# First batch's maxima split into two halves of eight heads, its second score pass started after the first half, GpSimd's bias sums moved behind its masks

## The chip, the cores and the metric

The kernel runs on one core of a Trainium2 chip. The metric is the device time of one execution in microseconds (us). The core's engines each run their own queue of instructions in order and wait for each other by semaphores: TensorE (PE in the rows; PEld is its loading of weights), VectorE (DVE), ScalarE (ACT), GpSimd (POOL) and SyncE (SP), which only starts DMAs. A trailing q (ACTq, SPq) marks the start of a DMA.

## The reference

The computation is one transformer layer on x of shape 8 x 256 x 256 (batch, token, feature), float32: cross attention to a context, then a layer of experts.

```python
scores = jnp.einsum('bihd,bjhd->bhij', qh, kh) * scale       # 16 heads of 16
keep = (j < i) | (i == 0) & (j == 0)
scores = jnp.where(keep, scores, jnp.float32(-jnp.inf))
probs = jax.nn.softmax(scores, axis=-1)
attn = jnp.einsum('bhij,bjhd->bihd', probs, vh).reshape(B, S, HID)
return attn @ W_o + b_o
...
x = x + _L0_xattn_ref(_layernorm(x), ctx, ctx, W_q, W_k, W_v, b_v, W_o, b_o)
x = x + _L0_ffn_ref(_layernorm(x), wg, w1, b1, w2, b2)       # top 2 of 8 experts, capacity 512
```

## The kernel before, in words

The attention part handles one batch per step, steps -2 to 8, as a software pipeline: in step s TensorE projects queries and keys of batch s+2, makes the maxima of batch s+1, and does the scores, exponentials and products with V of batch s. The order on every engine is written out by hand, in the `step` function of each engine's block and in the calls ahead of `steps(step)`; the first batch's maxima are in the calls ahead, its scores in step 0.

Queries and keys are cut into bf16 parts whose rows are stacked by DMAs into the buffers `Qs` and `Ks` (three of each; some share memory with expert weights, so the trace calls them `w_hi` and `w_lo`). A first score pass, `a_scores(s, pair)` (lines 1063 and 1066), puts twelve units of scores of batch s+1 into two banks in turn; units 0 to 5 are heads 0 to 7, units 6 to 11 heads 8 to 15. VectorE takes each unit's row maxima, negated (`maxima`, line 758); TensorE may score into a bank again when its maxima are taken.

`split_maxima` (lines 812, 814) then splits the 2 x 16 maxima per row into a bf16 part and the rest, TensorE turns them (`turn_maxima`, line 1161), ScalarE copies the result (`copy_maxima`, line 592) and starts a DMA (line 594) that puts them as two more rows into `Qs`. Since `Ks` holds ones in these rows, the second pass, `b_scores(s, g)` (lines 1079, 1082; four heads per group g), gives scores minus their maxima, which ScalarE's `exp` (line 525) turns into probabilities. GpSimd zeroes what the mask drops (`mask`, lines 395 to 397) and TensorE multiplies by V (`values`, lines 1098, 1099). The second pass uses banks 3 to 5; in the first batches bank 3 also takes the projected values of batch 0, which `add_value_bias(0)` moves into V with the bias added (line 775). Ahead of that it waits for V's ones, the extra column that yields the softmax's sum:

```python
dve.wait_ge(v_done, s + 2)
if first(s, 1):
    dve.wait_ge(ones_ready, s + 2)
```

`buffer_constants(q)` raises `ones_ready` on GpSimd (lines 315, 317). In GpSimd's queue, `buffer_constants(1)` follows `norm_powers(2)`, `fill_keys(2)` and `zero_queries(2)` (lines 320, 323: a memset of 128 x 2048 each); behind it come the context's split (line 404), the sums of x and the output's bias (`add_bias`, line 389) and the constants of the routing.

Of the kernel before, what the change touches and what calls it, by code (L numbers as in the profile page):

```python
# [6 lines left out]
P = 128  # L7
# [38 lines left out]
def attention(nc, sem, sb, persist, x, ctx_in, Wq, Wk, Wv, bv, Wo, bo, wg, w1, b1, w2, b2, xn_rows, out):  # L46
# [66 lines left out]
    nm_s = sb("nm_s", [P, 2, 2, HEADS], BF16)  # L113
    nmT = sb("nmT", [2 * HEADS, S], BF16)
    PT = [sb(f"PT{g}", [P, HPG * (S + P)], F32) for g in range(2)]
    OT = sb("OT", [P, GROUPS, S], F32)
# [42 lines left out]

    a_done, max_done, nm_ready, nmT_done, nmT_ready = (sem(n) for n in ("a_done", "max_done", "nm_ready", "nmT_done", "nmT_ready"))  # L160
    b_done, exp_done, mask_done, av_done, ot_ready = (sem(n) for n in ("b_done", "exp_done", "mask_done", "av_done", "ot_ready"))

# [73 lines left out]
    with block:  # L236
# [71 lines left out]
        def _(pool):  # L308
# [104 lines left out]
            def step(s):  # L413
                if s == 0:
                    add_bias(2)
                    mask(0, 0)
                    split_queries(0)
                    mask(0, 1)
                    split_keys(0)
                    mask(0, 2)  # L420
                    mask(0, 3)
                    norm_powers(3)
                    return
                if 0 < s < B - 2:
                    if s + 3 < B:
                        norm_powers(s + 3)
                    add_bias(s + 2)
                    split_context(s)
                    mask(s, 0)
                    mask(s, 1)  # L430
                    powers(s - 1, ln2_stats, mv2, ve2, rs2, ln2_pow)
                    split_keys(s)
                    mask(s, 2)
                    split_queries(s)
                    mask(s, 3)
                    return
# [38 lines left out]
            split_context(0)  # L475
            add_bias(0)
            add_bias(1)
            routing_constants()
            steps(step)
# [3 lines left out]
        def _(act):  # L483
# [104 lines left out]
            def copy_maxima(s):  # L588
                act.wait_ge(nmT_done, s + 2)
                if not first(s, 0):  # L590
                    act.wait_ge(max_stacked, 16 * (s + 1))
                act.activation(nmT[:, :], bank[1][0:2 * HEADS, 0:S], ACT.Copy).then_inc(nmT_ready, 1)
                wait_alone(act, started, nmT_ready, s + 2)
                act.dma_start(Qs[(s + 1) % BUFS][ROWS:ROWS + 2, :, :], nmT[:, :]).then_inc(max_stacked, 16)

            def step(s):
# [47 lines left out]
                else:  # L644
# [7 lines left out]
                    if proj_part(s) and s > 0:  # L652
                        round_x(s)
                    if s == 0:
                        round_queries(s)
                        exp(s, 0)
                        round_keys(s)
                        exp(s, 1)
                    elif score_part(s):
                        exp(s, 0)  # L660
                        exp(s, 1)
# [35 lines left out]
            round_queries(-1)  # L697
            round_context(0)
            norm_x(2)
            round_x(0)  # L700
            copy_maxima(-1)
            steps(step)

        @block.vector
        def _(dve):
# [46 lines left out]
            def unit_maxima(s, lo, hi):  # L752
                for u in range(lo, hi):
                    dve.wait_ge(a_done, UNITS * (s + 1) + u + 1)
                    if u == 0 and not first(s, 0):
                        dve.wait_ge(nm_ready, 2 * (s + 1))
# [46 lines left out]
            def logits(s):  # L803
                copy_logits(s)
                top_two(s - 1)

            def split_maxima(s):

                dve.wait_ge(max_done, UNITS * (s + 2))
                if not first(s, 0):  # L810
                    dve.wait_ge(nmT_done, s + 1)
                dve.tensor_copy(nm_s[:, :, 0, :], nm[:, :, :]).then_inc(nm_ready, 1)
                dve.wait_ge(nm_ready, 2 * (s + 1) + 1)
                dve.tensor_tensor(nm_s[:, :, 1, :], nm[:, :, :], nm_s[:, :, 0, :], ALU.subtract).then_inc(nm_ready, 1)
# [83 lines left out]
            def step(s):  # L898
# [71 lines left out]
                elif s == 0:  # L970
                    maxima(s, 0)
                    maxima(s, 1)
                    split_queries(s)
                    next_stats(s)
# [57 lines left out]
            next_stats(-1)  # L1032
            maxima(-1, 2)
            maxima(-1, 3)
            maxima(-1, 4)
            maxima(-1, 5)
            split_maxima(-1)
            add_value_bias(0)
            split_x(0)
# [5 lines left out]
        def _(pe):  # L1045
# [23 lines left out]
            def b_scores(s, g):  # L1069

                if g == 0:
                    pe.wait_ge(max_stacked, 16 * (s + 1))
                    if s == 0:
                        pe.wait_ge(v_ready, 2)
# [28 lines left out]
            def turn_values(s, t):  # L1103

                if t == 0:
                    pe.wait_ge(ot_ready, 2 * s)
                    if not (s > B - 1):
                        pe.wait_ge(nmT_ready, s + 1)
# [45 lines left out]
            def turn_maxima(s):  # L1154
                pe.wait_ge(nm_ready, 2 * (s + 2))
                if out_part(s):
# [3 lines left out]
                for t in range(2):  # L1160
                    last = pe.matmul(bank[1][0:2 * HEADS, t * P:(t + 1) * P], nm_s[:, t].rearrange("p a h -> p (a h)"), identb[:, :],
                                     start=True, stop=True)
                last.then_inc(nmT_done, 1)

            def project_turned(to, n, hi, lo, done):
# [21 lines left out]
            def queries(s):  # L1187
# [3 lines left out]
                elif out_part(s):  # L1191
                    pe.wait_ge(x2_ready, s)
                elif s == 0:
                    pe.wait_ge(nmT_ready, 1)
                project_turned(query_bank(s), 0, xT_hi, xT_lo, q_done)
# [72 lines left out]
            def step(s):  # L1268
                if s == B:
# [10 lines left out]
                    early_table(1, 1)  # L1280
                elif s == 0:
                    a_scores(s, 0)
                    queries(s)
                    b_scores(s, 0)
                    a_scores(s, 1)
                    keys(s)
                    b_scores(s, 1)
                    a_scores(s, 2)
                    values(s, 0)
                    a_scores(s, 3)  # L1290
                    b_scores(s, 2)
                    values(s, 1)
                    a_scores(s, 4)
                    b_scores(s, 3)
                    a_scores(s, 5)
                    values(s, 2)
                    turn_maxima(s)
# [131 lines left out]
            a_scores(-1, 2)  # L1429
            a_scores(-1, 3)  # L1430
            a_scores(-1, 4)
            turn_x(0)
            a_scores(-1, 5)
            turn_maxima(-1)
            steps(step)


# [478 lines left out]
```

## Time and profile before

| | us |
|---|---|
| median of 3 runs | 420.01 (419.99 to 422.09) |
| the profiled execution | 420.47 |
| its span, first to last instruction | 418.7 |
| TensorE busy | 365.2 (87%) |
| VectorE busy | 293.7 (70%) |
| ScalarE busy | 187.9 (45%) |
| GpSimd busy | 213.3 (51%) |

The attention stage takes the first half of the span, the experts the second. Shares of busy time are means over both. In the timelines below, a time in brackets at a row's end is how long the engine stood idle before it, with the instruction that ended the wait; a row without it followed at once, or nearly. The granted clock, PEclk, is 1.00 at the 2.4 GHz level and 0.50 at 1.2 GHz.

### The profile page before, as it was taken

Reading aid. Unit: us, or ns where it says so; the run is one execution under the profiler, and the core shown is the slowest. Engines: PE = TensorE matmul, PEld = TensorE weight load, DVE = VectorE, ACT = ScalarE, POOL = GpSimd, SP = SyncE. Lnnn points to the kernel's source line nnn. Section 1 sums busy time; section 2 is a strip of 40 time slices with the busy share of each in tenths; the row PEclk is TensorE's granted clock in tenths of the full one; section 3 lists DMA queues with packets and bytes.
Section 4 is the critical chain, followed back from the end, with each engine's and each line's share of the span. In section 5 each row is a group of like instructions: output and inputs, shape, how many; then the busy total and the mean of one; then the engine's idle time right before and its main releaser. Section 6 shows DMA issues by size and latency. Waiting matters only on the chain. (4 is left out here: it accounts for less than half of the span.)

```text
span 418.7 us, 8190 instructions
## 1 busy us (share of the span) xinstructions
PE 365.2 (87%) x3030; PEld 313.2 (75%) x3030; DVE 293.7 (70%) x627; ACT 187.9 (45%) x258; POOL 213.3 (51%) x305
## 2 busy tenths in 40 slices
PE   3777899999999999776418999999999999999991
PEld 3646597878787876545416899989899999989891
DVE  6586788887877777747733777776778777776840
ACT  4424556566665646751203436263625335263400
POOL 8679876767675635250446008163453717060632
PEclk9999999999999999995556999999999999999996
DMA  7774717162615172313218009173463809140323
GB/s 213 223 204 154 216 33 198 41 192 56 175 44 160 39 215 100 120 51 114 52 43 300 10 3 271 44 231 85 156 155 92 224 17 274 27 58 2 37 27 36
DMA packets 38315, 49.15 MB, mean 117 GB/s; under 512 B 7138, under 2 KB 34180, under 8 KB 37252
## 3 DMA queue, kind: packets, MB, share of 16 engines
q1 hardware_dynamic: 29636, 34.93, 28.0%
q0 software_dynamic: 6144, 8.33, 10.7%
q10 hardware_dynamic: 2496, 5.38, 4.0%
q8 instruction: 24, 0.39, 0.4%
q14 instruction: 15, 0.12, 0.1%
HBM read 27.60 MB, written 8.41 MB: 86 GB/s over the span
## 5 line engine op out<-in xcount | busy, mean ns | idle before, releaser
L1585 POOL DMA_INDIRECT out_dram<-Y,scatter_idx x32 | 51.3, 1603 | 105.8 <-DVE Y L1741 90.4
L1628 ACT ACTIVATE hr<-ps,b_sb 128x512 f32<-128x512 f32 x64 | 43.2, 686 | 98.9 <-PE ps L1785 65.1
L758 DVE TENSOR_REDUCE nm<-ps 128x2 f32<-128x512 f32 (+1 forms) x96 | 62.4, 682 | 15.3 <-PE ps L1066 14.7
L1795 PE MATMUL ps<-w_hi,h_hi 128*128 128x256 f32 x224 | 63.1, 282 | 0.0
L1795 PE MATMUL ps<-w_lo,h_hi 128*128 128x256 f32 x224 | 62.5, 279 | 0.0
L1795 PE MATMUL ps<-w_hi,h_lo 128*128 128x256 f32 x224 | 62.4, 279 | 0.0
L525 ACT ACTIVATE PT<-ps 128x1536 f32<-128x1536 f32 x32 | 46.4, 1451 | 26.7 <-PE ps L1082 26.2
L1716 DVE CAST h_hi<-hr 128x512 fp32r<-128x512 f32 x60 | 27.4, 456 | 38.9 <-ACT hr L1628 38.8
L1785 PE MATMUL ps<-XT_hi,w_hi 128*128 128x512 f32 x128 | 51.4, 402 | 1.5 <-DVE XT_lo L1699 1.5
L1785 PE MATMUL ps<-XT_hi,w_lo 128*128 128x512 f32 x128 | 51.2, 400 | 0.0
L1785 PE MATMUL ps<-XT_lo,w_hi 128*128 128x512 f32 x128 | 51.1, 399 | 0.0
L1795 PEld LDWEIGHTS ps<-w_hi,h_lo 128*128 128x128 f32 x224 | 42.1, 188 | 1.6
L1795 PEld LDWEIGHTS ps<-w_hi,h_hi 128*128 128x128 f32 x224 | 42.0, 188 | 1.5
L1718 DVE TENSOR_TENSOR h_lo<-hr,h_hi 128x512 fp32r<-128x512 f32 x60 | 41.7, 696 | 2.1
L1795 PEld LDWEIGHTS ps<-w_lo,h_hi 128*128 128x128 f32 x224 | 42.2, 188 | 0.0
L1572 POOL DMA_INDIRECT Xg<-xn_rows,gather_idx x32 | 32.4, 1014 | 12.4 <-issue 9.4
L1066 PE MATMUL ps<-mask,identb 128*128 128x256 bf16 (+1 forms) x96 | 29.7, 309 | 0.0
L1785 PEld LDWEIGHTS ps<-XT_hi,w_hi 128*128 128x128 f32 x128 | 24.5, 192 | 5.8 <-issue 1.9
L1785 PEld LDWEIGHTS ps<-XT_lo,w_hi 128*128 128x128 f32 x128 | 24.5, 192 | 5.8
L1785 PEld LDWEIGHTS ps<-XT_hi,w_lo 128*128 128x128 f32 x128 | 24.6, 192 | 3.8
L395 POOL TENSOR_SCALAR_AFFINE_SELECT PT<-PT 128x4 f32<-128x4 f32 x32 | 6.5, 204 | 33.3 <-ACT PT L525 33.2
L1098 PE MATMUL ps<-PT,V 128*32 128x256 f32 x256 | 21.5, 398 | 0.8 <-POOL PT L397 0.7
(234 smaller groups left out, 886.3 us busy)
## 6 DMA issues: line engine op xcount, KB each, us to landing
raw<-in_L_ffn_w_dram SPq DMA_DIRECT2D x12, 1024.0 KB, 8.1
raw<-in_L_ffn_w_dram ACTq DMA_DIRECT2D x4, 1024.0 KB, 5.3
c_sb<-in_ctx_dram SPq DMA_DIRECT2D x8, 256.0 KB, 3.2
xn_rows<-x2n SPq DMA_DIRECT2D x8, 256.0 KB, 3.2
out_dram<-x_all SPq DMA_DIRECT2D x8, 256.0 KB, 2.9
x_all<-in_x_dram SPq DMA_DIRECT2D x1, 1280.0 KB, 6.6
w_lo<-k_h SPq DMA_DIRECT2D x9, 128.0 KB, 2.5
w_hi<-q_h SPq DMA_DIRECT2D x9, 128.0 KB, 2.5
```

Source lines behind the costliest of these rows:

```text
L395: pool.affine_select(p0[:, :, 0:1], p0[:, :, 0:1], [[0, HPG], [0, 1]], ALU.is_ge, 0.0, base=0, channel_multiplier=-1)
L525: act.activation(PT[g % 2][:, :], prob_score, ACT.Exp, scale=float(HD) ** -0.5).then_inc(exp_done, 1)
L758: dve.tensor_reduce(nm[:, tile, h:h + count], max_bank[u % 2].rearrange("p (h j) -> p h j", h=count), AX_X, ALU.max, negate=True).then_inc ...
L1066: pe.matmul(diag, identb[:, :], mask1[:, :, :] if tile else mask0[:, :, :], start=False, stop=True, skip_group_check=True).then_inc(a_done, 1)
L1098: pe.matmul(out, V[s % 2][:, 0, h, :], PT[g % 2][:, hh * S:(hh + 1) * S], start=True, stop=False)
L1572: pool.indirect_dma_start(Xg[q][:, j, :], None, xn_rows[:, :], bass.IndirectOffsetOnAxis(ap=gather_idx[:, ST * e + j:ST * e + j + 1], axis ...
L1585: pool.indirect_dma_start(out_rows[:, :], bass.IndirectOffsetOnAxis(ap=scatter_idx[:, ST * e + j:ST * e + j + 1], axis=0), Y[q][:, j, :], ...
L1628: act.activation(hr[c % 2][:, :], h_bank[c % 4], ACT.Relu, bias=b1_sb[q][:, c:c + 1]).then_inc(hr_ready, 1)
L1716: dve.tensor_copy(h_hi_of(e, c), hr[c % 2][:, :]).then_inc(hh_ready, 1)
L1718: dve.tensor_tensor(h_lo_of(e, c), hr[c % 2][:, :], h_hi_of(e, c).bitcast(F32), ALU.subtract).then_inc(hl_ready, 1)
L1785: last = pe.matmul(h_bank[c % 4], w[q][:, k, c, :], a[q][:, k, :], start=(n == 1), stop=(n == 6))
L1795: last = pe.matmul(y_bank[j // 2][:, (j % 2) * D:(j % 2 + 1) * D], a[c % 4][:, j * P:(j + 1) * P], w[q][:, c, :], start=(c == 0 and n == 0 ...
```

## The change

The first batch's maxima are split, turned and stacked in two halves. `split_half(0)` follows the sixth maximum and `split_half(1)` the twelfth; `turn_half` and `copy_half` do for eight heads what `turn_maxima` and `copy_maxima` do for sixteen, each with buffers and semaphores of its own. The second score pass of groups 0 and 1 waits for the first half's DMA, that of groups 2 and 3 for the second's. `add_value_bias(0)` is moved ahead of the second half's maxima, since `b_scores(0, 0)`, which writes over its bank, now comes earlier. The order of step 0 is written anew on TensorE, VectorE, ScalarE and GpSimd. GpSimd's `add_bias` of batches 0, 1 and 2 and its routing constants come later. In the other batches only the counts of the semaphores are one lower.

```diff
@@ pool.step @@
                 if s == 0:
-                    add_bias(2)
                     mask(0, 0)
+                    add_bias(0)
                     split_queries(0)
                     mask(0, 1)
                     split_keys(0)
                     mask(0, 2)
                     mask(0, 3)
                     norm_powers(3)
+                    add_bias(1)
+                    add_bias(2)
                     return
+                if s == B - 2:
+                    routing_constants()
@@ pool, ahead of the steps @@
             buffer_constants(1)
             split_context(0)
-            add_bias(0)
-            add_bias(1)
-            routing_constants()
             steps(step)
@@ act @@
+            def copy_half(n):
+                act.wait_ge(half_nmT_done, n + 1)
+                act.activation(nmT_half[n][:, :], bank[1][0:HEADS, n * S:(n + 1) * S], ACT.Copy).then_inc(half_nmT_ready, 1)
+                act.wait_ge(half_nmT_ready, n + 1)
+                act.dma_start(Qs[0][ROWS:ROWS + 2, n * HEADS // 2:(n + 1) * HEADS // 2, :], nmT_half[n][:, :]).then_inc(half_stacked[n], 16)
...
                     if s == 0:
+                        exp(s, 0)
+                        copy_half(1)
                         round_queries(s)
-                        exp(s, 0)
+                        exp(s, 1)
                         round_keys(s)
-                        exp(s, 1)
...
             round_context(0)
+            copy_half(0)
             norm_x(2)
             round_x(0)
-            copy_maxima(-1)
             steps(step)
@@ dve @@
+            def split_half(n):
+                heads = slice(n * HEADS // 2, (n + 1) * HEADS // 2)
+                dve.wait_ge(max_done, (n + 1) * UNITS // 2)
+                dve.tensor_copy(nm_half[:, n, :, 0, :], nm[:, :, heads]).then_inc(half_nm_ready, 1)
+                dve.wait_ge(half_nm_ready, 2 * n + 1)
+                dve.tensor_tensor(nm_half[:, n, :, 1, :], nm[:, :, heads], nm_half[:, n, :, 0, :], ALU.subtract).then_inc(half_nm_ready, 1)
...
                     maxima(s, 0)
+                    split_queries(s)
                     maxima(s, 1)
-                    split_queries(s)
...
             maxima(-1, 2)
+            split_half(0)
+            add_value_bias(0)
             maxima(-1, 3)
             maxima(-1, 4)
             maxima(-1, 5)
-            split_maxima(-1)
-            add_value_bias(0)
+            split_half(1)
             split_x(0)
             steps(step)
@@ pe @@
             def b_scores(s, g):
 
+                if s == 0 and g % 2 == 0:
+                    pe.wait_ge(half_stacked[g // 2], 16)
...
+            def turn_half(n):
+                pe.wait_ge(half_nm_ready, 2 * n + 2)
+                pe.wait_ge(k_rest_ready, 2)
+                if n == 1:
+                    pe.wait_ge(half_nmT_ready, 1)
+                for t in range(2):
+                    last = pe.matmul(bank[1][0:HEADS, n * S + t * P:n * S + (t + 1) * P], nm_half[:, n, t].rearrange("p a h -> p (a h)"), identb[:, :],
+                                     start=True, stop=True)
+                last.then_inc(half_nmT_done, 1)
...
             def queries(s):
                 elif s == 0:
-                    pe.wait_ge(nmT_ready, 1)
+                    pe.wait_ge(half_nmT_ready, 2)
...
                 elif s == 0:
+                    b_scores(s, 0)
+                    turn_half(1)
                     a_scores(s, 0)
                     queries(s)
-                    b_scores(s, 0)
+                    b_scores(s, 1)
                     a_scores(s, 1)
+                    values(s, 0)
                     keys(s)
-                    b_scores(s, 1)
                     a_scores(s, 2)
-                    values(s, 0)
+                    b_scores(s, 2)
                     a_scores(s, 3)
-                    b_scores(s, 2)
                     values(s, 1)
+                    b_scores(s, 3)
                     a_scores(s, 4)
-                    b_scores(s, 3)
+                    values(s, 2)
                     a_scores(s, 5)
-                    values(s, 2)
                     turn_maxima(s)
                     values(s, 3)
...
             a_scores(-1, 3)
+            turn_half(0)
             a_scores(-1, 4)
             turn_x(0)
             a_scores(-1, 5)
-            turn_maxima(-1)
             steps(step)
```

On VectorE the order around the first batch's maxima was this (the reduces write `nm`; the cast and the subtraction that follow make `nm_s`; the V row is the value bias, the last row the split of x):

```order
L758 TENSOR_REDUCE nm<-ps 128x2
L758 TENSOR_REDUCE nm<-ps 128x4
L758 TENSOR_REDUCE nm<-ps 128x2 x2
L758 TENSOR_REDUCE nm<-ps 128x4
L758 TENSOR_REDUCE nm<-ps 128x2 x2
L758 TENSOR_REDUCE nm<-ps 128x4
L812 CAST nm_s<-nm 128x2x16
L814 TENSOR_TENSOR nm_s<-nm,nm_s 128x2x16
L775 TENSOR_TENSOR V<-ps,bv_bc 128x32x16
L725 TENSOR_TENSOR xT_lo<-ps,xT_hi 128x512
```

The same place on VectorE is now, with line numbers of the changed kernel (its V row is again the value bias):

```order
L772 TENSOR_REDUCE nm<-ps 128x2
L772 TENSOR_REDUCE nm<-ps 128x4
L824 CAST nm_half<-nm 128x2x8
L826 TENSOR_TENSOR nm_half<-nm,nm_half 128x2x8
L789 TENSOR_TENSOR V<-ps,bv_bc 128x32x16
L772 TENSOR_REDUCE nm<-ps 128x2 x2
L772 TENSOR_REDUCE nm<-ps 128x4
L772 TENSOR_REDUCE nm<-ps 128x2 x2
L772 TENSOR_REDUCE nm<-ps 128x4
L824 CAST nm_half<-nm 128x2x8
L826 TENSOR_TENSOR nm_half<-nm,nm_half 128x2x8
L737 TENSOR_TENSOR xT_lo<-ps,xT_hi 128x512
```

The value bias has moved from behind the twelve maxima to behind the sixth, ahead of six reduces.

On TensorE, from the last scores of the first batch to the queries of step 0, the order was this (the row with `nm_s` turns the maxima, the rows with `Ks,Qs` and `mask` are the next batch's scores):

```order
L1063 MATMUL ps<-w_lo,w_hi 128x128 x4
L1066 MATMUL ps<-mask,identb 128x512
L1161 MATMUL ps<-identb,nm_s 32x128 x2
L1063 MATMUL ps<-Ks,Qs 128x256 x2
L1066 MATMUL ps<-mask,identb 128x2x128
L1063 MATMUL ps<-Ks,Qs 128x256 x2
L1066 MATMUL ps<-mask,identb 128x2x128
L1172 MATMUL ps<-xT_hi,w_hi 128x256
```

It is now this, where lines 1106 and 1109 are the second score pass of group 0 and line 1198 turns the second half:

```order
L1087 MATMUL ps<-w_lo,w_hi 128x128 x4
L1090 MATMUL ps<-mask,identb 128x512
L1106 MATMUL ps<-w_hi,w_lo 128x256 x4
L1109 MATMUL ps<-w_hi,w_lo 128x128 x4
L1198 MATMUL ps<-identb,nm_half 16x128 x2
L1087 MATMUL ps<-Ks,Qs 128x256 x2
L1090 MATMUL ps<-mask,identb 128x2x128
L1087 MATMUL ps<-Ks,Qs 128x256 x2
L1090 MATMUL ps<-mask,identb 128x2x128
L1209 MATMUL ps<-xT_hi,w_hi 128x256
```

The second pass of group 0 has moved ahead of the turning, of a pair of score units and of the queries' twelve matmuls.

## Rows read from the trace of the kernel before

**Rows 1.** Waits of TensorE, 49.8 to 150 us: total, times, longest.

```profile
PE ps L1079 <- DMA w_lo<-nmT: 0.9, 1, 0.9
```

**Rows 2.** Timeline of VectorE, 25 to 49 us: start, duration, instruction, [idle before].

```profile
25.80 3.94 DVE L758 TENSOR_REDUCE nm<-ps 128x2 f32<-128x512 f32 x6
...
30.04 1.29 DVE L758 TENSOR_REDUCE nm<-ps 128x2 f32<-128x512 f32 x2 [0.29 <-PE ps L1066]
...
32.02 0.69 DVE L775 TENSOR_TENSOR V<-ps,bv_bc 128x512 f32<-128x512 f32 x1
...
37.66 1.29 DVE L758 TENSOR_REDUCE nm<-ps 128x4 f32<-128x512 f32 x2 [3.15 <-PE ps L1066]
...
38.87 0.68 DVE L733 TENSOR_TENSOR q_rest<-ps,q_h 128x512 f32<-128x512 f32 x1
...
47.87 0.53 DVE L814 TENSOR_TENSOR nm_s<-nm,nm_s 128x32 bf16<-128x32 f32 x1
```

**Rows 3.** Timeline of GpSimd, 27 to 32 us, same columns.

```profile
27.72 1.80 POOL L320 MEMSET w_hi<- 128x2048 f32 x1
...
31.78 0.15 POOL L317 MEMSET V<- 128x32 f32 x1
```

**Rows 4.** Timeline of TensorE, 32 to 50 us, same columns.

```profile
32.04 0.28 PE L1161 MATMUL ps<-identb,nm_s 128*32 128x128 bf16 x2 [1.60 <-DVE nm_s L814]
...
33.37 0.38 PE L1172 MATMUL ps<-xT_hi,w_hi 128*128 128x256 f32 x1 [0.28 <-DVE xT_lo L725]
...
36.35 0.61 PE L1079 MATMUL ps<-w_hi,w_lo 128*128 128x256 bf16 x4 [1.30 <-DMA w_hi<-nmT]
...
37.71 0.36 PE L1172 MATMUL ps<-cT_hi,w_hi 128*128 128x256 f32 x1
...
39.21 0.61 PE L1079 MATMUL ps<-w_hi,w_lo 128*128 128x256 bf16 x4
...
41.56 0.39 PE L1063 MATMUL ps<-Ks,Qs 126*128 126x256 bf16 x2
...
46.96 0.66 PE L1098 MATMUL ps<-PT,V 128*32 128x256 f32 x8
...
48.45 0.29 PE L1161 MATMUL ps<-identb,nm_s 128*32 128x128 bf16 x2 [0.61 <-DVE nm_s L814]
...
49.01 0.66 PE L1098 MATMUL ps<-PT,V 128*32 128x256 f32 x8 [0.27 <-POOL PT L397]
...
49.82 0.39 PE L1183 MATMUL ps<-w_hi,cT_hi 128*128 128x256 f32 x1
```

**Rows 5.** Timeline of ScalarE, 32 to 38 us, same columns.

```profile
32.36 0.37 ACT L592 ACTIVATE nmT<-ps 32x256 bf16<-32x256 f32 x1 [2.06 <-PE ps L1161]
...
35.08 0.60 ACT L503 ACTIVATE q_h<-ps 128x512 bf16<-128x512 f32 x1 [2.35 <-PE ps L1172]
...
37.22 1.45 ACT L525 ACTIVATE PT<-ps 128x1536 f32<-128x1536 f32 x1 [1.54 <-PE ps L1082]
```

**Rows 6.** Timeline of GpSimd, 33 to 56 us, same columns.

```profile
33.10 2.51 POOL L389 TENSOR_TENSOR x_all<-x_all,bo_bc 128x512 f32<-128x512 f32 x2
...
43.36 0.61 POOL L330 CAST k_m<-k_rest 128x512 bf16<-128x512 f32 x1
...
45.49 0.20 POOL L395 TENSOR_SCALAR_AFFINE_SELECT PT<-PT 128x4 f32<-128x4 f32 x1
...
55.40 0.21 POOL L395 TENSOR_SCALAR_AFFINE_SELECT PT<-PT 128x4 f32<-128x4 f32 x1 [0.36 <-ACT PT L525]
```

**Rows 7.** Busy time by stretch: PE, PEld, DVE, ACT, POOL; PEclk, DMA share, GB/s.

```profile
17.90:20.90 3.00, 0.30 (x4) 0.10 (x3) 1.82 (x3) 0.00 (x0) 1.04 (x2) 1.00 0.77 196
...
184.00:186.00 2.00, 1.16 (x20) 0.69 (x18) 0.94 (x1) 1.73 (x2) 0.62 (x2) 1.00 0.76 262
...
186.00:188.00 2.00, 2.00 (x23) 1.53 (x23) 0.79 (x8) 0.00 (x0) 0.80 (x2) 0.64 0.00 0
```

**Rows 8.** Busy time by stretch, the experts' first matmuls, columns as before.

```profile
223.00:227.00 4.00, 4.00 (x10) 3.13 (x11) 0.97 (x4) 0.69 (x1) 2.82 (x4) 0.50 0.92 369
```

More of the change, by code:

```diff
@@ L114, in attention @@
     nmT = sb("nmT", [2 * HEADS, S], BF16)
+    nmT_half = [sb(f"nmT_half{n}", [HEADS, S], BF16) for n in range(2)]
+    nm_half = sb("nm_half", [P, 2, 2, 2, HEADS // 2], BF16)
     PT = [sb(f"PT{g}", [P, HPG * (S + P)], F32) for g in range(2)]
@@ L160, in attention @@
     a_done, max_done, nm_ready, nmT_done, nmT_ready = (sem(n) for n in ("a_done", "max_done", "nm_ready", "nmT_done", "nmT_ready"))
+    half_nm_ready, half_nmT_done, half_nmT_ready = sem("half_nm_ready"), sem("half_nmT_done"), sem("half_nmT_ready")
+    half_stacked = [sem(f"half_stacked{n}") for n in range(2)]
     b_done, exp_done, mask_done, av_done, ot_ready = (sem(n) for n in ("b_done", "exp_done", "mask_done", "av_done", "ot_ready"))
@@ L588, in copy_maxima @@
             def copy_maxima(s):
-                act.wait_ge(nmT_done, s + 2)
-                if not first(s, 0):
-                    act.wait_ge(max_stacked, 16 * (s + 1))
+                act.wait_ge(nmT_done, s + 1)
+                if s > 0:
+                    act.wait_ge(max_stacked, 16 * s)
                 act.activation(nmT[:, :], bank[1][0:2 * HEADS, 0:S], ACT.Copy).then_inc(nmT_ready, 1)
-                wait_alone(act, started, nmT_ready, s + 2)
+                wait_alone(act, started, nmT_ready, s + 1)
                 act.dma_start(Qs[(s + 1) % BUFS][ROWS:ROWS + 2, :, :], nmT[:, :]).then_inc(max_stacked, 16)
+            def copy_half(n):
[3 more added lines that the diff above has]
+                act.dma_start(Qs[0][ROWS:ROWS + 2, n * HEADS // 2:(n + 1) * HEADS // 2, :], nmT_half[n][:, :]).then_inc(half_stacked[n], 16)
             def step(s):
@@ L754, in unit_maxima @@
                     dve.wait_ge(a_done, UNITS * (s + 1) + u + 1)
-                    if u == 0 and not first(s, 0):
-                        dve.wait_ge(nm_ready, 2 * (s + 1))
+                    if u == 0 and s == 0:
+                        dve.wait_ge(half_nm_ready, 4)
+                    if u == 0 and s > 0:
+                        dve.wait_ge(nm_ready, 2 * s)
                     tile, h, count = max_unit(u)
@@ L805, in logits @@
                 top_two(s - 1)
+            def split_half(n):
[4 more added lines that the diff above has]
+                dve.tensor_tensor(nm_half[:, n, :, 1, :], nm[:, :, heads], nm_half[:, n, :, 0, :], ALU.subtract).then_inc(half_nm_ready, 1)
             def split_maxima(s):
                 dve.wait_ge(max_done, UNITS * (s + 2))
-                if not first(s, 0):
-                    dve.wait_ge(nmT_done, s + 1)
+                if s == 0:
+                    dve.wait_ge(half_nmT_done, 2)
+                else:
+                    dve.wait_ge(nmT_done, s)
                 dve.tensor_copy(nm_s[:, :, 0, :], nm[:, :, :]).then_inc(nm_ready, 1)
-                dve.wait_ge(nm_ready, 2 * (s + 1) + 1)
+                dve.wait_ge(nm_ready, 2 * s + 1)
                 dve.tensor_tensor(nm_s[:, :, 1, :], nm[:, :, :], nm_s[:, :, 0, :], ALU.subtract).then_inc(nm_ready, 1)
@@ L1069, in b_scores @@
             def b_scores(s, g):
+                if s == 0 and g % 2 == 0:
+                    pe.wait_ge(half_stacked[g // 2], 16)
                 if g == 0:
-                    pe.wait_ge(max_stacked, 16 * (s + 1))
+                    if s > 0:
+                        pe.wait_ge(max_stacked, 16 * s)
                     if s == 0:
@@ L1107, in turn_values @@
                     if not (s > B - 1):
-                        pe.wait_ge(nmT_ready, s + 1)
+                        pe.wait_ge(nmT_ready, s)
                 elif max_part(s):
@@ L1154, in turn_maxima @@
             def turn_maxima(s):
-                pe.wait_ge(nm_ready, 2 * (s + 2))
+                pe.wait_ge(nm_ready, 2 * (s + 1))
                 if out_part(s):
```

## The prediction, on record before the changed kernel ran

> **What bounds the kernel now.** I read the table of stages first, then the waits of TensorE, then the timelines of the engines around the change. From the second batch on TensorE hardly waits: between 49.8 and 150 us its longest wait is 0.9 us [rows 1]. So the attention stage from 50 us on runs at TensorE's pace, and whatever the first batch's step ends earlier or later by reaches the end of the span nearly whole. The change lies before that, between 27 and 50 us, where TensorE does wait: 1.60 us for the split maxima, then 1.30 us for the DMA that stacks them [rows 4]. VectorE waits there once, 3.15 us, and from 37.66 on its queue runs without a gap until 47.87 + 0.53 = 48.40 [rows 2]: 10.74 us of work.
>
> I call the units of the first batch's maxima u6 to u11 in its second half, b(0,g) the second score pass of group g in step 0, and "end of step 0" the first values projection of step 1, at 49.82 [rows 4].
>
> **The change part by part.**
>
> *Splitting by halves, and the V bias.* On VectorE the first half's split stands behind the sixth maximum, and right behind it now stands the addition of the value bias into V, ahead of u6. This addition waits for `ones_ready`, which GpSimd raises with its second filling of V's ones. The filling isn't moved: it starts at 31.78 and takes 0.15, so it is done at 31.93; ahead of it GpSimd runs two large memsets, of 1.80 us each, the first from 27.72 [rows 3]. Those start when the norm's powers are done, which hang on statistics whose place on VectorE is the same. In the kernel before, the addition started at 32.02, and the wait was met by then [rows 2].
>
> Now VectorE is there at about 27.8 (the six maxima from 25.80 take 3.94, so the second of them ends at 27.11; the split pair behind it is my estimate of 0.7). It stands until 31.95, over 4 us, and behind it in its queue are u6 to u11, for which TensorE waits: each of its score units but the next two needs a bank that a maximum frees. With the addition's 0.69, u6 starts at 32.65 instead of 27.11: **5.5 us later**. Everything up to the second half's turning moves with it: u11 ends at 31.33 + 5.5 = 36.85, the second turning is at 32.04 + 5.5 = 37.55. TensorE is done with the last scores at 32.04 - 1.60 + 5.5 = 35.95 and starts b(0,0) there, 0.4 before the 36.35 of before. The first half's rows are long in place: from turning to b(0,0) it was 36.35 - 32.04 = 4.31 [rows 4], so from 27.9 they land at 32.2. This is all that the early half gains.
>
> *The second half's copy.* It stands behind exp(0,0) on ScalarE, and queries(0) wait for it. Exp started 37.22 - 36.35 = 0.87 behind b(0,0) and takes 1.45; the copy took 0.37 [rows 5]. So: 35.95 + 0.87 + 1.45 + 0.37 = 38.65, queries at 38.7 instead of 33.37. A projection of this size takes 39.21 - 37.71 = 1.5 [rows 4], so b(0,1) starts at 40.2 (before 39.21), and the rounded queries come 35.08 - 33.37 = 1.71 later and take 0.60: at 41.0. VectorE's split of the queries starts at 41.05; before, 38.87 [rows 2].
>
> *What follows in step 0.* Two bounds. From below: with no further wait, the 10.74 us of VectorE run from 41.05 to 51.8 (the two maxima that stood ahead of the queries' split are behind it now, so all of it counts), and the turning that was at 48.45 is at 51.85. Before, the last products waited 0.27 for their mask behind that turning [rows 4]; that wait goes, so step 0 ends 3.4 - 0.27 = 3.1 later. From above, the chain through the keys: they now stand behind b(0,1), a pair of score units and a group of products, a set that took 41.56 - 39.21 = 2.35 [rows 4]. So keys at 42.55, the next pair of scores at 44.05, its first unit 0.4 later (half of a third of 2.35, an estimate) at 44.45; VectorE would have been there before, so it waits. Two maxima (1.31) and the keys' split (0.68, as the queries') end at 46.45; GpSimd's mask of the third group starts 45.49 - 43.36 = 2.13 behind its first piece of the keys [rows 6], at 48.6, and the products 46.96 - 45.49 = 1.47 behind that, at 50.1 instead of 46.96. The last pair of scores is now behind these products: 0.8 + 0.4 (thirds of 2.35 again), then the last two maxima, which in the first batch started 2.00 before their turning (30.04 to 32.04): 51.3 + 2.0 = 53.3, against 48.45, or 4.85 - 0.27 = 4.6 at the end of step 0. Consecutive instructions overlap by about 0.1, which this addition counts in several places, so I take **4.4**, near the upper end.
>
> *The clock.* During VectorE's stop TensorE has nothing but the small turning of the first half from about 27.6 to 33.3. A stretch of 3.00 us with 0.30 busy left the granted clock at 1.00 (the 2.4 GHz level); later 1.16 busy of 2.00 us was followed by a fall to 0.50 (1.2 GHz), the mean of the next 2 us being 0.64 [rows 7]. This stop would be nearly twice the first of these stretches and emptier than the second, so I expect the fall. Once down, TensorE was busy for 4.00 us of 4.00 and still at 0.50 [rows 8]. Half rate over such a stretch loses at most 2.0; at least 0, if the clock holds. Part of it lies under VectorE's maxima, but b(0,0) and the turning of x don't, so I take **1.5**, towards the upper end. The Trainium skill, page "TensorE: Matmul & The Clock Gate", section "HAM oscillation — how this bites in real kernels", says that a matmul burst after a long wait begins throttled, every time; by it the fall is sure and the sum is the one above, and the first of rows 7 speaks neither for nor against it, being shorter.
>
> *Edits that I cost at nothing.* GpSimd's bias sums for batches 1 and 2, 2.51 us for two [rows 6], go behind the norm's powers at the end of step 0. GpSimd leaves its masks some 2.5 later than before (its third is 3.1 late, and the fourth had had to wait a little), plus 2.51, so it comes to the first mask of step 1 about 5.0 later; that mask had 0.36 of wait for exp, and exp itself comes 4.4 later, so 0.2 is left, ahead of products that stand behind a projection; without this cover it would be those 2.51. The first bias sum, half of 2.51, stands behind the first mask, where GpSimd waits for the queries' remainder anyway. The routing constants go to the last step but one, into GpSimd's wait for that step's first exp. One DMA issue and a copy more on ScalarE lie in its waits before the norm and before the rounded queries. The first half's two VectorE instructions lie inside the stop.
>
> **Sum.** 4.4 + 1.5 = 5.9. The profiled execution took 420.47; with it 426.4. It lies 0.46 above the median of 420.01, so the forecast is **425.9**.
>
> **The rivals.**
>
> *The clock holds.* For it: 0.30 busy in 3.00 us did nothing [rows 7]. Against: the length of this stop. Time: 420.0 + 4.4 = 424.4.
>
> *The clock falls again at the end of step 0.* There TensorE waits for the third mask and for the last maxima, and a thin stretch preceded the fall at 186 [rows 7]. Step 1, which TensorE bounds, would then begin at half rate: 2.0 more [rows 8], 427.9. Against: in the same place before, it held with somewhat fewer waits.
>
> *VectorE is never behind.* The chain through the keys finds slack that I don't see, and only VectorE's 10.74 us count: 3.1 and no clock, 423.1.
>
> *The other side: V's ones are there in time.* If GpSimd's two memsets were much shorter with VectorE standing still, VectorE would pass the addition at 27.8, u6 would start at 28.5, 1.4 late; b(0,0) would wait for its rows until 32.2, the queries come at 34.95, their split on VectorE at 37.3, and 10.74 later, 48.05, the turning: 0.4 earlier, and 0.27: 419.3. Each us of stop costs one us, so it is later than before from 0.7 us of stop on. For it: nothing but that the early half is there to be used. Against: the memset took 1.80 [rows 3], and both would have to vanish.
>
> **How the numbers follow.** Forecast 0.42, clock holds 0.27, clock falls twice 0.16, VectorE's floor 0.08, ones in time 0.05, 0.02 for anything else. Half a per cent, 2.1 us, is about what a measurement here can tell from no change. All cases but the fifth lie over 422.1: slower 0.93. The fifth gives 419.3 at its best, which is inside: same 0.05, faster 0.02. The range from 422.8 to 428.4 holds the floor, the forecast and the second fall with half a us to spare on either side.
>
> **What would show it.** In the profile after: an idle time of about 4 us on VectorE before the line that adds the value bias, at 32 us, put down to GpSimd's memset of V; TensorE without scores from 28 to 33 us; b(0,0) at about 36, queries near 38.7 (later, if the clock fell: then PEclk is 0.50 from some 32 us to 38); the end of step 0 at 54 to 56 instead of 49.82; from there every stage shifted alike. The prediction is wrong if VectorE does not stop there, if step 1 starts before 52, or if a later stage gives time back.

## The result, and the profile after

The changed kernel took 425.68 us (median of 6 runs, 423.36 to 429.64); the kernel before, run beside it, 422.05 (419.99 to 424.29). The ratio is 1.0103, 95% interval [1.0068, 1.0139]: on 420.01 us, 4.3 us slower (2.9 to 5.8). The forecast was 425.9, which is 5.9 slower. The profiled execution took 423.36, span 421.6.

Times ahead of the change differ between executions (the third pair of the first batch's maxima starts at 25.40 here, at 25.80 in before [rows 2]). So I count from the start of that pair, called **u4**; each such time is from one profiled execution. The end of step 0 (the first values projection of step 1) lies 24.02 behind u4 in before, 29.27 in after: **5.25 us later**.

VectorE after, timeline from 25 us on (start, duration, instruction, idle before and its releaser):

```profile
25.40 1.25 DVE L772 TENSOR_REDUCE nm<-ps 128x2 f32<-128x512 f32 x2
...
26.89 0.17 DVE L826 TENSOR_TENSOR nm_half<-nm,nm_half 128x16 bf16<-128x16 f32 x1
31.62 0.69 DVE L789 TENSOR_TENSOR V<-ps,bv_bc 128x512 f32<-128x512 f32 x1 [4.56 <-POOL V L321]
32.23 1.28 DVE L772 TENSOR_REDUCE nm<-ps 128x2 f32<-128x512 f32 x2
...
```

The stop is there: VectorE stands 4.56 us ahead of the value bias, and the seventh maximum, u6, starts at 32.23, 6.83 behind u4. In before it came 1.31 behind [rows 2]. What it waits for stands in GpSimd's timeline of after:

```profile
27.31 1.80 POOL L324 MEMSET w_hi<- 128x2048 f32 x1
29.06 1.81 POOL L327 MEMSET w_lo<- 128x2048 f32 x1
30.80 0.53 POOL L319 MEMSET V<- 128x512 f32 x1
31.38 0.15 POOL L321 MEMSET V<- 128x32 f32 x1
...
42.09 0.61 POOL L334 CAST q_m<-q_rest 128x512 bf16<-128x512 f32 x1 [0.62 <-DVE q_rest L745]
...
46.87 0.61 POOL L334 CAST k_m<-k_rest 128x512 bf16<-128x512 f32 x1 [1.54 <-DVE k_rest L745]
...
60.45 0.21 POOL L399 TENSOR_SCALAR_AFFINE_SELECT PT<-PT 128x4 f32<-128x4 f32 x1
```

The two large memsets still stand ahead of V's ones, as in before [rows 3]. The last row is step 1's first mask: no wait is listed, and GpSimd comes to it late, but no wait of TensorE for it follows (below). TensorE after, timeline 27 to 55 us:

```profile
27.14 0.28 PE L1198 MATMUL ps<-identb,nm_half 128*16 128x128 bf16 x2
32.97 0.61 PE L1087 MATMUL ps<-w_lo,w_hi 126*128 126x128 bf16 x4 [5.55 <-DVE nm L772]
...
36.35 0.60 PE L1106 MATMUL ps<-w_hi,w_lo 128*128 128x256 bf16 x4
...
37.87 0.28 PE L1198 MATMUL ps<-identb,nm_half 128*16 128x128 bf16 x2 [0.70 <-DVE nm_half L826]
...
39.06 0.36 PE L1209 MATMUL ps<-xT_hi,w_hi 128*128 128x256 f32 x1
...
40.51 0.61 PE L1106 MATMUL ps<-w_hi,w_lo 128*128 128x256 bf16 x4
...
50.60 0.66 PE L1125 MATMUL ps<-PT,V 128*32 128x256 f32 x8 [1.47 <-POOL PT L401]
...
53.74 0.28 PE L1188 MATMUL ps<-identb,nm_s 128*32 128x128 bf16 x2 [1.38 <-DVE nm_s L837]
...
54.67 0.39 PE L1220 MATMUL ps<-w_hi,cT_hi 128*128 128x256 f32 x1
```

Of the waits of before that the halves were to shorten [rows 4], the 1.30 for the stacking DMA is gone, and of the 1.60 for the split 0.70 is left. In their place stands one of 5.55, and in step 0 one of 1.47 for the third mask (none before) and one of 1.38 for the last maxima (0.61 before). The clock, by stretches of after (TensorE, weight load, VectorE, ScalarE, GpSimd busy; granted clock; DMA share, GB/s):

```profile
28.00:32.00 4.00, 0.00 (x0) 0.00 (x0) 0.38 (x1) 1.09 (x2) 3.94 (x5) 0.63 0.89 265
32.00:36.00 4.00, 3.03 (x17) 2.41 (x18) 2.84 (x5) 0.46 (x1) 0.74 (x1) 0.52 0.57 187
36.00:40.00 4.00, 3.16 (x30) 2.40 (x29) 3.53 (x7) 1.84 (x3) 1.20 (x3) 1.00 0.01 2
40.00:55.00 15.00, 12.15 (x148) 8.88 (x148) 11.34 (x24) 6.52 (x7) 12.22 (x21) 1.00 0.66 177
```

It fell during the stop to the lower level (1.2 GHz), held there through three of the four score units that were left, and was back at 36. It did not fall again before 55. From step 1 on (53 to 153 us) TensorE waits as little as before [rows 1]. Apart from the wait at 53.74, the longest is:

```profile
PE ps L1106 <- DMA w_lo<-nmT: 0.4, 1, 0.4
```

### The profile page after: what moved, and what is told of

The parts are those of the page before. It is cut to its first block and busy times, and to the rows that moved or that the text cites. A ratio compares the mean times of both kernels' runs of the same rounds, so it can differ in the third digit from the quotient of the medians.

```text
span 421.6 us, 8198 instructions
## 1 busy us (share of the span) xinstructions
PE 364.1 (86%) x3032; PEld 312.6 (74%) x3032; DVE 293.6 (70%) x629; ACT 188.3 (45%) x259; POOL 213.6 (51%) x305
## 5 line engine op out<-in xcount | busy, mean ns | idle before, releaser
L772 DVE TENSOR_REDUCE nm<-ps 128x2 f32<-128x512 f32 (+1 forms) x96 | 62.3, 681 | 14.4 <-PE ps L1090 14.0
L1087 PE MATMUL ps<-w_lo,w_hi 126*128 126x256 bf16 (+1 forms) x96 | 14.3, 256 | 10.1 <-DVE nm L772 7.0
```

The costliest lines, as they stand in the source:

```text
L1087: pe.matmul(max_bank[u % 2][:, h * width:(h + 1) * width], Q[0:ROWS, h0 + h, tile * P:(tile + 1) * P], K[0:ROWS, h0 + h, 0:width], start=( ...
```

## The experiments

A time "behind u4" can be compared between kernels; a ratio is against the kernel before, run beside it on the same chip.

**1. V's ones early.** GpSimd fills them ahead of the norm's powers and of the two large memsets; the rest is as after.

```diff
             split_queries(-1)
+            buffer_constants(1)
             norm_powers(2)
...
             zero_queries(2)
-            buffer_constants(1)
             split_context(0)
```

> The changed kernel with one call moved: GpSimd fills V's ones for batch 1 before the third norm's powers instead of behind its two large memsets. If VectorE's stop at the value bias is what costs, the stop is gone, the sixth maximum is followed by the second half within 1.5 us, the clock stays at 1.00, and step 1 begins at 49.1 to 50.6 us of the span (54.67 in the changed kernel, 49.82 before); the time is within 0.3% of the kernel before. If it is the new order of step 0 that costs, step 1 still begins at 52 us or later.

Measured: 423.94 us, ratio 1.0011 [0.9975, 1.0047]. VectorE has no stop any more (its timeline):

```profile
28.44 0.17 DVE L826 TENSOR_TENSOR nm_half<-nm,nm_half 128x16 bf16<-128x16 f32 x1
28.55 0.69 DVE L789 TENSOR_TENSOR V<-ps,bv_bc 128x512 f32<-128x512 f32 x1
```

But the end of step 0 is 27.02 behind u4: 2.25 less than in after, and still 3.00 later than before. It lies at 53.97 of the span, past the 52 that was the sign for the new order. TensorE's timeline shows two reasons:

```profile
28.69 0.28 PE L1198 MATMUL ps<-identb,nm_half 128*16 128x128 bf16 x2
...
34.98 1.03 PE L1106 MATMUL ps<-w_hi,w_lo 128*128 128x256 bf16 x4 [1.58 <-DMA w_hi<-nmT_half]
...
49.91 0.66 PE L1125 MATMUL ps<-PT,V 128*32 128x256 f32 x8 [1.47 <-POOL PT L401]
...
53.05 0.28 PE L1188 MATMUL ps<-identb,nm_s 128*32 128x128 bf16 x2 [1.38 <-DVE nm_s L837]
```

The half's rows need 34.98 - 28.69 = 6.29 from turning to use, where before needed 4.31 [rows 4], and the clock falls about the end of that wait:

```profile
31.00:34.00 3.00, 1.43 (x12) 1.04 (x12) 1.84 (x4) 1.52 (x3) 2.63 (x2) 1.00 0.99 339
34.00:38.00 4.00, 3.02 (x16) 1.78 (x16) 1.69 (x5) 1.52 (x2) 0.00 (x0) 0.58 0.28 72
```

(Stretches of the same execution; the DMA engines are 0.99 busy in the first. That this delays the rows fits, but was not tried by itself; in experiment 8 the rows were in use 4.56 after the turning.) And the new order's waits of 1.47 and 1.38 are the same as in after. The stop was the largest single cause that was taken out, not the only one. (The ratio's interval ends at 2.0 us, under the 3.00 of this one execution; how often the clock falls there is not known.)

**2. The stop with TensorE kept busy.** After, with 23 matmuls into an unused bank while VectorE stands.

```diff
             turn_half(0)
+            for _ in range(23):
+                pe.matmul(ps[:, 4, :], identb[:, :], mask0[:, :, :].rearrange("p h j -> p (h j)"), start=True, stop=True)
             a_scores(-1, 4)
```

> The changed kernel with 23 unused matmuls of 128x512 on TensorE during VectorE's stop, into a bank that is free then. If the fall of the clock costs what was predicted, the granted clock stays at 1.00 from 27 to 37 us and step 1 begins 1.0 to 1.8 us earlier than 54.67. If the fall lies wholly under VectorE's maxima, step 1 begins within 0.3 us of 54.67.

Measured: 428.23 us, ratio 1.0072 [1.0027, 1.0118]. Its clock around the stop, columns as above:

```profile
29.00:37.00 8.00, 6.71 (x36) 2.96 (x36) 3.38 (x9) 1.46 (x3) 6.67 (x9) 1.00 0.60 181
```

VectorE's stop is as long, and behind it the six maxima run without a gap (its timeline):

```profile
35.23 0.69 DVE L789 TENSOR_TENSOR V<-ps,bv_bc 128x512 f32<-128x512 f32 x1 [4.55 <-POOL V L321]
35.84 4.08 DVE L772 TENSOR_REDUCE nm<-ps 128x2 f32<-128x512 f32 x6
```

The clock holds at 2.4 GHz, and the end of step 0 is 28.33 behind u4: 4.31 later than before. So of after's 5.25 the clock made 29.27 - 28.33 = **0.94**, a little under the 1.0 to 1.8 expected, and the stop and the order 4.31. (The profiled execution was the longest of this kernel's, 431.04 us, but from 26 us to the end of step 0 its granted clock is 1.00 throughout. The totals alone, 1.0072 and 1.0103, are too close to tell the two kernels apart.)

**3. The bias early, alone.** Before, with only the value bias moved ahead of the seventh maximum: no halves, no new order.

```diff
             maxima(-1, 2)
+            add_value_bias(0)
             maxima(-1, 3)
...
             split_maxima(-1)
-            add_value_bias(0)
             split_x(0)
```

> The kernel before, whole maxima and old order, with only the value bias moved ahead of the second half's maxima on VectorE. If the stop costs by itself, VectorE waits over 4 us for V's ones and step 1 begins at 53.5 to 56 us instead of 49.82. If the 3.15 us that VectorE waits later in the kernel before can take the stop up, step 1 begins before 51.5 us.

Measured: 426.7 us, ratio 1.0101 [1.0061, 1.0141], the same loss as the whole change. VectorE's stop, and then TensorE's timeline:

```profile
32.69 0.69 DVE L775 TENSOR_TENSOR V<-ps,bv_bc 128x512 f32<-128x512 f32 x1 [4.97 <-issue]
```

```profile
34.04 0.61 PE L1063 MATMUL ps<-w_lo,w_hi 126*128 126x128 bf16 x4 [5.75 <-DVE nm L758]
...
56.02 0.38 PE L1183 MATMUL ps<-w_hi,cT_hi 128*128 128x256 f32 x1
```

"issue" names no releaser; GpSimd's memset of V's ones runs from 32.45 to 32.60, so it is the same wait. The clock falls here too (0.50 from 34 to 38 us). With u4 at 26.47, step 0 ends 5.53 later. One moved line is enough to make the loss.

**4. GpSimd's moves, alone.** Before, with `add_bias(0)` between the first mask and the queries' split, `add_bias(1)` and `(2)` behind `norm_powers(3)`, and the routing constants in the last step but one:

```diff
                 if s == 0:
-                    add_bias(2)
                     mask(0, 0)
+                    add_bias(0)
                     split_queries(0)
...
                     norm_powers(3)
+                    add_bias(1)
+                    add_bias(2)
                     return
...
```

> The kernel before with only GpSimd's bias sums and routing constants moved as in the change. If they are hidden, as predicted, step 1 begins at 49.6 to 50.1 us and its first products are not late. If the sums delay the masks or the next context's split, TensorE waits for GpSimd in step 0 or 1, by 0.8 to 2.5 us in all.

Measured: 424.62 us, ratio 1.003 [0.9991, 1.0068]; the end of step 0 is 1.84 later (25.86 behind u4). Where it shows on TensorE:

```profile
45.30 0.66 PE L1099 MATMUL ps<-PT,V 128*32 128x256 f32 x8 [2.09 <-POOL PT L397]
```

In before it was this:

```profile
43.47 0.66 PE L1098 MATMUL ps<-PT,V 128*32 128x256 f32 x8 [0.41 <-POOL PT L397]
```

In the old order GpSimd has no slack ahead of the queries' split, so `add_bias(0)` pushes its masks. In after it waits 0.62 and 1.54 at the two splits, and the same edit costs nothing there.

**5. The old waits filled, without halves.** Before, with the keys, and VectorE's statistics and splits, put into the wait for the DMA; GpSimd's splits ahead of its masks. TensorE's part:

```diff
                     queries(s)
+                    keys(s)
                     b_scores(s, 0)
                     a_scores(s, 1)
-                    keys(s)
                     b_scores(s, 1)
...
```

> The kernel before without any halves; only the order of step 0 is new: TensorE does the keys ahead of the second score pass, in the 1.30 us that it waits for the stacked maxima; VectorE does statistics and both splits in its 3.15 us of wait; GpSimd splits the queries ahead of the first mask; the bias sum of batch 2 and the routing constants come later. If step 0 is bound by waits that an order can fill, step 1 begins at 48.0 to 49.0 us (49.82 before) and the time falls by 0.2 to 0.4%. If only an earlier second pass can help, as the change has it, step 1 begins at 49.6 or later.

Measured: 422.5 us, ratio 1.0023 [0.9994, 1.0052]; 1.26 later at the end of step 0. The expectation missed: the wait for the DMA went, and these took its place (waits of TensorE, 34 to 53 us):

```profile
PE ps L1099 <- POOL PT L397: 2.0, 3, 0.9
PE ps L1080 <- ACT PT L526: 0.8, 1, 0.8
PE ps L1162 <- DVE nm_s L815: 0.8, 1, 0.8
```

Step 0 is paced by VectorE and GpSimd as well as by that wait; work put into it comes out behind it.

**6. After, once more**, with no edit.

> The changed kernel once more, beside the others on one chip. The first 6 runs gave a ratio of 1.0103, and its profile gave 2 us back between 186 and 204 us, where the clock fell later than in the profile before. If that gift belongs to the execution and not to the kernel, the mean ratio is near 1.012 (5.3 us at the end of step 0); if a later stage takes the delay up for good, it is at most 1.007.

Measured: 426.73 us, ratio 1.0109 [1.0069, 1.015]. This is nearer to the first expectation (1.012) than to the second (at most 1.007). The end of step 0 is again 29.27 behind u4, to the hundredth. What differs is the stretch from the last but one turning of x2 to the experts' first matmul, in which the attention ends and the routing is done. The first row is of after, the second of this execution, the third of before:

```profile
187.79:225.83 38.04, 16.79 (x158) 12.13 (x159) 22.06 (x72) 8.16 (x15) 14.07 (x19) 0.66 0.30 82
```

```profile
189.24:229.57 40.33, 20.17 (x158) 14.55 (x159) 22.17 (x72) 8.15 (x15) 14.04 (x19) 0.55 0.27 77
```

```profile
183.48:222.97 39.49, 18.82 (x158) 13.64 (x159) 22.18 (x72) 8.16 (x15) 14.06 (x20) 0.54 0.29 80
```

One program took 38.04 and 40.33 for the same 158 matmuls, at mean clocks of 0.66 and 0.55. So the 1.45 us that after's profile gives back there against before (39.49 - 38.04) can't be put down to the change. In this execution nothing is given back: its span is 425.4, 6.7 over the 418.7 of before.

**7 and 8. Halves with another step 0.** Both build on experiment 1, with `add_bias(0)` ahead of the first mask. In 7 the keys go ahead of the queries on every engine, the weights' split behind the maxima; in 8 step 0 has before's order from the queries on. TensorE's part of 7:

```diff
                     a_scores(s, 0)
-                    queries(s)
+                    keys(s)
                     b_scores(s, 1)
                     a_scores(s, 1)
+                    queries(s)
                     values(s, 0)
-                    keys(s)
                     a_scores(s, 2)
...
```

And of 8:

```diff
                     queries(s)
-                    b_scores(s, 1)
                     a_scores(s, 1)
-                    values(s, 0)
                     keys(s)
+                    b_scores(s, 1)
                     a_scores(s, 2)
-                    b_scores(s, 2)
+                    values(s, 0)
...
```

> The changed kernel with V's ones filled early (as in the first experiment) and step 0 ordered anew: keys ahead of the queries on all engines, so that TensorE has work while the second half's copy waits behind the first exp; the weights' split and a memset behind the maxima. If the halves are worth something once nothing waits for V's ones and the copy is covered, step 1 begins 22 to 23.5 us after the maxima of the third pair begin (24.02 before, 29.27 in the changed kernel). If the halves' DMA or VectorE's queue bounds it, 24 us or more.

> The changed kernel with V's ones filled early and, from the queries on, the order of step 0 of the kernel before on TensorE, ScalarE, VectorE and GpSimd. Between the end of the first group's scores, the first pair and the queries on TensorE and the start of step 1 lay 12.80 us before and 14.16 in the changed kernel. If the new order costs the 1.4 us between them, 12.6 to 13.1 here; if they come from the lateness of what stands ahead, 14 or more again.

Measured: 7 took 421.45 us, ratio 1.0007 [0.9979, 1.0035], end of step 0 23.81 behind u4 (0.21 earlier than before, between its two expectations); 8 took 423.99, ratio 1.0045 [1.0025, 1.0065], though its step 0 ends 23.02 behind u4, a whole 1.00 earlier. Once the queries, the second pass of group 0 and the first pair of score units are issued, the same work is left up to step 1 in all three orders: it took 54.67 - 40.51 = 14.16 in after, 49.82 - 37.02 = 12.80 in before and 49.03 - 36.53 = 12.50 in 8 (TensorE's timelines; one row of before, two of 8):

```profile
37.02 0.39 PE L1063 MATMUL ps<-Ks,Qs 126*128 126x128 bf16 x4
```

```profile
36.53 0.84 PE L1087 MATMUL ps<-Ks,Qs 126*128 126x128 bf16 x6
...
49.03 0.39 PE L1220 MATMUL ps<-w_hi,cT_hi 128*128 128x256 f32 x1
```

In experiments 1 and 2, which have after's order and other times ahead of it, the same work took 53.97 - 39.82 = 14.15 and 57.34 - 43.18 = 14.16. So the new order costs 1.4, and it is the order, not the halves nor the lateness of what stands ahead. But 8 pays in step 1 (its TensorE timeline):

```profile
53.67 0.38 PE L1087 MATMUL ps<-w_hi,w_lo 126*128 126x256 bf16 x2 [2.55 <-issue]
```

"issue" names no releaser. The last key transfer was started at 47.43, and the list of DMA issues, 30 to 60 us (KB each, median us to landing), puts its landing at 47.43 + 6.2 = 53.63, where TensorE starts:

```profile
raw<-in_L_ffn_w_dram ACTq DMA_DIRECT2D x1, 1024.0 KB, 9.3
...
w_hi<-k_l SPq DMA_DIRECT2D x1, 128.0 KB, 6.2
```

The first row is 1 MB of expert weights, started at 42.63, so it lands at 51.93, while that transfer is under way. The clock falls right behind TensorE's wait:

```profile
49.00:53.60 4.60, 2.12 (x20) 1.85 (x16) 1.28 (x3) 2.27 (x4) 4.14 (x7) 1.00 0.22 52
53.60:57.00 3.40, 3.33 (x21) 2.85 (x22) 1.44 (x4) 0.71 (x1) 2.95 (x4) 0.57 0.00 0
```

**9 to 11. That load later.** The 1 MB goes to the end of step 0 in 8 (run 9), in 7 (run 10) and in before (run 11, the control).

```diff
-                    if s in (0, B - 3):
-                        prefetch(s != 0)
+                    if s == B - 3:
+                        prefetch(1)
...
                     if max_part(s) and s > 0:
                         copy_maxima(s)
+                    if s == 0:
+                        prefetch(0)
```

> The halves with GpSimd's ones early and step 0 in its old order (the run before this one in its line), and now the 1 MB load of the experts' weights that ScalarE issues at 42.6, in the middle of step 0, comes after the last instruction of step 0 on ScalarE (about 48 to 49). Theory: step 1's first score pass waited 2.55 us at 53.67 for the second part of the stacked keys, whose last transfer took 6.2 us from issue to landing beside that load. Without it the transfers take 3 us or so, the wait is under 0.6, and the lead of 1.0 us at the end of step 0 is kept: the turning of x2 at 120.8 to 121.8 after the third pair's maxima (before 122.25, without the move 124.89), total 419.5 to 421.5 where before gives 422. Rival: the wait is the late split of the keys and not the load: it stays over 2 us, and the total is as without the move, 423.5 to 424.5.

> The halves with GpSimd's ones early and the keys ahead of the queries throughout, and the same load moved to the end of step 0. There the wait for the stacked queries at 53.16 was only 0.79. Theory: that wait goes and nothing else, so 0.5 to 1 us below the kernel without the move, total 420.5 to 421.5. Rival: no change within what a measurement tells (421.5 +- 1).

> The kernel before with the same load alone moved to the end of step 0: the control for the two others. Its step 1 waits only 0.2 us for stacked parts, so no change is expected: ratio 0.998 to 1.002. Rival: the load later gets in the way of step 1's own stacking, and the ratio is above 1.002.

Measured: 9 took 424.42 us, ratio 1.0048 [1.0008, 1.0087]; 10 took 423.57, 1.003 [0.9996, 1.0064]; 11 took 422.41, 0.9998 [0.996, 1.0035]. The mechanism is right: in 9 the key transfer lands in 2.4, and TensorE's wait of 2.55 in step 1 is gone:

```profile
raw<-in_L_ffn_w_dram ACTq DMA_DIRECT2D x1, 1024.0 KB, 4.8
...
w_hi<-k_l SPq DMA_DIRECT2D x1, 128.0 KB, 2.4
```

From step 1 to the first turning of x2 it takes 152.34 - 53.16 = 99.18, against 101.87 in 8 and 98.23 in before. The 0.95 over before is a new wait, for step 1's first mask (TensorE's timeline):

```profile
62.31 0.66 PE L1127 MATMUL ps<-PT,V 128*32 128x256 f32 x8 [0.95 <-POOL PT L401]
```

GpSimd works without a pause up to that mask, and in its queue stand the two bias sums, 2.52 us, that the change moved to the end of step 0. So where TensorE isn't late by something else, that edit shows (read from the rows; it was not tried by itself). In 10 this wait is 0.52.

The total I expected of 9, 419.5 to 421.5, is not there: it is the rival's (423.5 to 424.5), but not for the rival's reason. 10 lies over both ranges that were given for it, and 11 came as expected. The end of step 0 is 24.78 behind u4 in 9, 24.42 in 10 and 24.24 in 11. That of 9 is 1.76 later than in 8, with the same order ahead of it. The same stretch in 9 and (second row) in 8:

```profile
32.00:39.00 7.00, 6.24 (x31) 3.80 (x31) 4.30 (x8) 3.35 (x5) 4.37 (x5) 0.51 0.36 116
```

```profile
32.00:39.00 7.00, 5.86 (x56) 5.16 (x55) 5.72 (x11) 2.72 (x5) 3.34 (x5) 1.00 0.50 162
```

All of the 1.76 is there by the queries (9.03 behind u4 in 8, 39.18 - 28.38 = 10.80 in 9), before the moved load starts (53.33). Of the five profiled executions with V's ones early the clock fell about there in four (0.58 from 34 to 38 us in experiment 1 and from 31 to 35 in 7, 0.51 in 9, 0.50 from 32 to 37 in 10) and held only in 8. So the lead of 1.00 in 8 is that of the one execution in which it held. How often it falls is not known from one profile each, so why 9 and 10 gain nothing in the median stays open. No run beat the kernel before.

## Why the prediction was right

The mechanism held, and so did its chain, step by step. Times behind u4: as predicted without the clock term (the prediction's times less 25.80; for step 1 with the 4.4 that it took), as measured with the clock held (experiment 2), and in after:

| start of | predicted | clock held | after |
|---|---|---|---|
| value bias on VectorE | 6.15 | 6.22 | 6.22 |
| second pass of group 0 | 10.15 | 10.02 | 10.95 |
| queries | 12.9 | 12.72 | 13.66 |
| second pass of group 1 | 14.4 | 14.17 | 15.11 |
| third group's products | 24.3 | 24.26 | 25.20 |
| last turning | 27.5 | 27.40 | 28.34 |
| step 1 | 28.4 | 28.33 | 29.27 |

That the total came out at 425.68 against 425.9 is in part luck: the kernel before took 422.05 beside it, not the 420.01 that the forecast starts from, so the medians are 3.63 apart and not 5.9.

- *The stop*: over 4 us and u6 5.5 later were forecast; 4.56 and 6.83 - 1.31 = 5.52 measured. Experiment 1 removes the cause and the stop goes; experiment 3 makes it alone.
- *Step 0's order*: of the bounds 3.1 and 4.6 I took 4.4; with the clock held it was 4.31. The chain through the keys was the right one: the two waits that it gives, for the third mask and for the last maxima, are rows of after.
- *The clock*: the fall came, at the place named; its size failed. I took 1.5 of at most 2.0; it cost **0.94**. The low stretch in which TensorE had work ran only from 32.97 to about 36, not 4 us, and part of it lay under VectorE's maxima, which at full clock (experiment 2) set the pace there. What the Trainium skill says (page "TensorE: Matmul & The Clock Gate", section "HAM oscillation — how this bites in real kernels"), that a burst after a long wait begins throttled, fits after and experiments 3 and 6: behind waits of 5.55, 5.75 and 5.54 the clock was 0.52, 0.50 and 0.50.
- *Edits at nothing*: true where they stand. GpSimd came to step 1's first mask 5.45 later behind u4 than before (5.0 forecast), and no wait of TensorE followed. But the cover was the change's own lateness: by experiment 4 `add_bias(0)` costs 1.84 without the wait for the queries' remainder, and in 9, by the rows, the two other sums cost 0.95. My reasons for both were the right ones.
- *"If a later stage gives time back"*: in the profiled execution 5.25 at step 1 became 423.36 - 420.47 = 2.89 at the end. I had named that as a sign against me. Of the 2.36 between them, 0.40 is a lead that this execution had already at u4 (25.40 against 25.80); 0.54 lies between step 1 and the last but one turning of x2 (133.12 against 133.66 in before), and 1.45 in the stretch with the routing behind it. In experiment 6 the same program took 134.11 and 40.33 for these two, more than before in both, so what was given back is that of one execution. Over all runs, 4.3 [2.9 to 5.8] and, by experiment 6, 4.6 are left of the 5.25; whether part of it is really given back is inside the interval and stays open. The forecast's 5.9 was 0.65 over the 5.25: 0.56 of clock and 0.09 of chain.
- *The rivals*: with the clock held it would be +4.31 at step 0, as that rival said (4.4), but it fell; it did not fall again (1.00 from 40 to 55, and from 55 to 60); VectorE's floor of 3.1 was not reached, since TensorE waits for masks and maxima that the keys hold up. Experiment 1 builds "V's ones in time": its step 0 ended 3.00 later, not 0.7 earlier, since my price left out a slower landing of the rows, the clock's fall in that wait, and the new order's 1.4.

So after's 5.25 splits into 1.4 of new order, 0.94 of clock and, by the remainder, 2.9 of stop, net of what the early half saved. The stop alone, in the old order and with its clock, costs 5.53.

## What to carry to other kernels

Before an instruction is moved up in a queue that runs in order, look up when each of its semaphores was raised in the trace, and what stands ahead of the one that raises it: here a 0.15 us memset behind two of 1.80 made a stop of 4.56. What is cheap in one order may not be in another: cost a moved edit against the waits that will be there after the change, and try it alone. Compare stages from a marker next to the change; a difference of the whole span takes in clock changes that have nothing to do with it.

## What the runs showed that was not expected

- TensorE's clock falls in some executions and not in others at the same place of the same order: 1.00 in experiment 8 and 0.51 in 9, from the half's turning on, worth 1.76 us; and the routing stretch of one program took 38.04 and 40.33 us.
- Two of GpSimd's sums, hidden in after, stand ahead of a wait of 0.95 us in experiment 9, where step 0 ends earlier.
- A transfer of 128 KB took 6.2 us from issue to landing beside a 1 MB load and 2.4 without it; the load itself took 9.3 and 4.8.
